# A transformer layer on eight cores: what TensorE waits for at the start of each group of heads

## The reference

```
a = layernorm(x)
Q = (a @ Wq.T + bq) * 128**-0.25 ; K = (a @ Wk.T + bk) * 128**-0.25 ; V = a @ Wv.T + bv
o = softmax(causal(Q @ K.T)) @ V            # head by head
x = x + layernorm(o @ Wo.T + bo)
h = bitlinear(layernorm(x), w_up)           # 2048 -> 4096
x = x + layernorm(bitlinear(relu(h)**2, w_down))
# bitlinear: activations quantised to 8 bits a row, weights to -1/0/1 times mean(|w|)
```

## Time and profile before

| | us |
|---|---|
| median of 2 runs | 6040.78 |
| the two runs | 6040.31 and 6041.24 |
| the profiled execution, its own time | 6060.33 |
| its span (slowest core, core 3) | 6058.8 |
| fastest core's span (core 0) | 5947.7 |

### The profile page before, as it was taken

How to read it: one execution, slowest core, us unless ns; L and a number is a source line. 1 busy time by engine, 2 the same in 40 slices (tenths; PEclk the granted TensorE clock), 3 DMA queues, 4 the chain that set the end, 5 groups by cost and what they waited for, 6 DMA issues and landing times.

```text
span 6058.8 us, 34280 instructions; the slowest of 8 cores (5947.7 to 6058.8 us)
## 1 busy us (share of the span) xinstructions
PE 2888.8 (48%) x10388; PEld 1096.4 (18%) x10388; DVE 1890.7 (31%) x2752; ACT 824.2 (14%) x929; POOL 378.2 (6%) x712
## 2 busy tenths in 40 slices
PE   0000474444744445644437444427847746675376
PEld 0000121111311112211113111102313312232132
DVE  1145022111131111212221311123456365363663
ACT  1100001111001112011110011110011112111210
POOL 0001110000110000100001100010000000000000
PEclk9999967766867777777778676657868868788688
DMA  5677421100121111201101110212134444433443
GB/s 92 99 224 233 92 43 35 39 32 33 39 60 35 35 35 34 49 35 35 35 35 39 46 35 35 89 61 103 49 104 115 118 132 111 157 108 97 130 114 118
DMA packets 358264, 471.07 MB, mean 78 GB/s; under 512 B 161473, under 2 KB 317121, under 8 KB 337345
## 3 DMA queue, kind: packets, MB, share of 16 engines
q0 software_dynamic: 68944, 251.21, 14.8%
q1 hardware_dynamic: 289138, 217.66, 13.3%
HBM read 385.39 MB, written 83.36 MB: 77 GB/s over the span
## 4 chain that ended last, share of the span: by engine, by line
PE 38%; DVE 17%; DMA 16%; ACT 12%; issue 6%; DVEq 4%; SPq 3%; POOL 3%; ACTq 0%; POOLq 0%
PE psB L1051 6%; ACT pt L643 6%; PE psB L473 4%; PE psB L435 4%; PE psB L1177 4%; PE psB L557 3%; DMA xt<-x 3%; DMA wqch<-wdnt 3%; DMA wqch<-wupt 3%; PE psB L795 3%; PE psB L664 2%; DVE tq_bf L387 2%; DMA qfm_ar<-qtile 2%; PE psB L505 2%; PE psA L630 2%
## 5 line engine op out<-in xcount | busy, mean ns | idle before, releaser
L1051 PE MATMUL psB<-wsl_f,qfm_ar 128*128 128x512 bf16 x2048 | 483.3, 401 | 350.0 <-DMA qfm_ar<-qtile 350.0
L1177 PE MATMUL psB<-wsl_f,qfm_ar 128*128 128x512 bf16 x2048 | 493.6, 406 | 267.4 <-DMA qfm_ar<-qtile 221.0
L643 ACT ACTIVATE pt<-psA,negC 128x1024 bf16<-128x1024 f32 x320 | 356.6, 1114 | 711.0 <-PE psA L634 708.7
L664 PE MATMUL psB<-pt,ones_bf 128*128 128x512 bf16 x320 | 149.8, 468 | 586.7 <-DVEq L91 325.8
L583 PE MATMUL psB<-sq_t,ones_f 128*128 128x512 f32 x128 | 89.4, 787 | 686.8 <-DVEq L91 686.8
L653 DVE TENSOR_TENSOR pt<-pt,strip 128x512 bf16<-128x512 bf16 x256 | 97.5, 422 | 1000.7 <-ACT pt L643 1000.7
L435 PE MATMUL psB<-y_fm,wsl 128*128 128x512 bf16 x1024 | 240.9, 402 | 180.2 <-DVEq L91 125.3
L1051 PEld LDWEIGHTS psB<-wsl_f,qfm_ar 128*128 128x128 bf16 x2048 | 208.3, 102 | 625.1 <-issue 409.4
L1177 PEld LDWEIGHTS psB<-wsl_f,qfm_ar 128*128 128x128 bf16 x2048 | 209.6, 103 | 551.3 <-issue 343.2
L795 PE MATMUL psB<-wo_bf,y_fm 128*128 128x512 bf16 x1024 | 268.4, 429 | 61.6 <-DVEq L91 55.3
L296 PE MATMUL psB<-smallA,ones_f 128*1 128x4 f32 x2 | 0.2, 166 | 623.8 <-DVEq L91 623.8
(11 more groups left out here) (160 smaller groups left out, 3232.1 us busy)
## 6 DMA issues: line engine op xcount, KB each, us to landing
wsl_f<-tup_sp SPq DMA_DIRECT2D x512, 128.0 KB, 2.7
wsl_f<-tdn_sp SPq DMA_DIRECT2D x512, 128.0 KB, 2.8
wch<-wupt POOLq DMA_DIRECT2D x16, 2048.0 KB, 9.0
wch<-wdnt POOLq DMA_DIRECT2D x32, 1024.0 KB, 5.5
wqch<-wupt POOLq DMA_DIRECT2D x32, 1024.0 KB, 5.6
wqch<-wdnt POOLq DMA_DIRECT2D x32, 1024.0 KB, 5.7
xt<-x SPq DMA_DIRECT2D x16, 1024.0 KB, 12.3
tup_sp<-tq_bf POOLq DMA_DIRECT2D x128, 128.0 KB, 2.2
```

Of the source, the lines that this page charges most:

```text
L643: exp_done[(hq, u)] = p.op("scalar", lambda e, sb=sb: e.activation(out=p_t[sb][:], in_=S2[sb][:, 0:1024], func=ACT.Exp, bias=negC[:], scal ...
L664: p.op("tensor", lambda e, sb=sb, u=u: e.matmul(PS[5][:, :], ones_bf[:, :], p_t[sb][:, 0:512], start=(u == 0), stop=False))
L1051: t_mm = p.op("tensor", lambda e, par=par, c=c, t=t, j=j: e.matmul(PS[par][:, :], q1fm[:, c * 512 + t * 128: c * 512 + (t + 1) * 128], wsl ...
L1177: t_mm = p.op("tensor", lambda e, par=par, c=c, t=t, s=s: e.matmul(PS[par][:, :], q2fm[:, c * 512 + t * 128: c * 512 + (t + 1) * 128], wsl ...
```

## The change

The two waits at the head of a group are replaced. For group 0 there is none. For the later groups TensorE waits for the reciprocal and for the output of the last attention block of the group before, and no longer for all that VectorE has been given.

```
@@ -411,8 +411,9 @@
     q_proj_last = {}
     hq = 0
     for grp in range(NG):
-        p.wait("tensor", SA, p.n(SA))
-        p.wait("tensor", SV, p.n(SV))
+        if grp > 0:
+            p.wait("tensor", SA, a_rec[hq - 1])
+            p.wait("tensor", SV, o_evac[hq - 1])
         wsl = wsl2[grp % 2]
         if grp == 0:
             lk = None
```

## The result

The changed kernel takes 5948.2 us in the median of 11 runs (5926.6 to 6039.1), the kernel before 6050.7 us in the median of 10 (6039.0 to 6109.1). The ratio is 0.9826 with a 95% interval of 0.9790 to 0.9861: 1.74% faster. The forecast was 5924.0 with a range up to 5942.0, so the time came out 24.2 us above the forecast and 6.2 us above the range. Ratios and means over the cores leave out executions in a second, slower state (one die over 1% longer than the other at a lower clock, or a time over 1.5% above the fastest), while medians and ranges hold all: without its one such execution, of 6039.1 us, the changed kernel's median is 5945.6, still 3.6 us above the range.

A forecast was written before the change was run, and what follows sets the result against it. The prediction took the kernel to be bound by waits, with TensorE's K projection held by VectorE at three group boundaries. Gains of 39.48, 38.63 and 38.72 us sum to 116.8; 6040.8 - 116.8 = 5924.0 us, range 5908 to 5942.

The forecast's parts named there:

- The stall and its releaser: At three group boundaries the K projection waited 125.3 us on VectorE, released by the third FFN-weight quantisation.
- Rival (d): Another event ending at the same time holds the K projection, so the time stays 6040.8 us; chance 0.02.
- The sum of 116.8 us: Gain from starting the K projection after the last attention output: 39.48, 38.63 and 38.72 us at the three boundaries.
- The moved work at nothing: Three quantisations under the K projection cost nothing, GpSimd issuing their last store 15.8 us before V weight loads are wanted.
- Rival (b): Contention stretches quantisations beyond the K projection, V loads 13 us late in all; gain 103.8, time 5937.0 us; chance 0.10.
- The slow start stays: The K projection still begins with eight matmuls at the low clock, costing 1.65 us per boundary as before.
- rival (a): With the gap gone, the K projection's slow start vanishes too: 121.7 us gained, time 5919.1 us; chance 0.13.
- a rise that comes later: At the K projection's start, a clock rise later than now was the only way to lose there; no size given.
- Rival (c): The whole K projection stays at the low clock, 49.8 us more per boundary; time 6073.4 us; chance 0.03.
- The base of the sum: Whole kernel's time before the edit, taken as the runs' median of 6040.8 us, from which the gain was subtracted.
- The range: Whole kernel's time between 5908 and 5942 us, with a few microseconds allowed for the spread between executions.
- The classes: Chances for the whole kernel: faster by over 2% 0.32, within 2% 0.66, slower by over 2% 0.02.

The follow-up runs named there:

- a fourth unit: Changed kernel with four FFN-weight quantisations instead of three at each group boundary, taken from the end of the attention stage; ratio 0.9730 to the kernel before.
- the fifth: Changed kernel with five FFN-weight quantisations instead of three at each group boundary, taken from the end of the attention stage; ratio 0.9764 to the kernel before.
- The filled gap: Kernel before with its wait kept and 170 thrown-away matmuls in TensorE's idle time at each boundary; ratios 1.0028 and 1.0014 to the kernel before.
- the three later comparisons: The changed kernel measured again, unedited, three times against the kernel before; ratios 0.9825, 0.9777 and 0.9799.

## Why the prediction missed, point by point

**The stall and its releaser: right.** The third quantisation held the K projection, and without it the projection starts 0.33 to 0.42 us after the output of the last block at each boundary of each core. Rival (d) falls.

**The sum of 116.8 us: right within what can be measured.** The trace shows 116.0 of waiting gone on core 7, 115.2 +- 2.8 in the means over the cores, 0.9813 (0.9790 to 0.9836) in the ratios against 0.9807 forecast. The time followed the wait when part of it was put back.

**The moved work at nothing, with a slack of 15.8 us: right.** GpSimd stood idle for 15.47 us; a fourth unit was all but free, the fifth was late. Rival (b) falls.

**The slow start stays: right, though it is 0.5 us longer at each boundary; rival (a) falls.** The projection began at 0.50 and took 58.1 us where the rows of before give 57.7. The prediction named this case, a rise that comes later, and put nothing on it. The filled gap shows the start from another side. On core 3 of its second profile dense matmuls ran at 1.00 up to 3.02 us ahead of the projection, and the projection still began at 0.50:

```profile
1500.00:1520.00 20.00, 20.00 (x94) 9.08 (x93) 4.78 (x3) 0.00 (x0) 5.33 (x10) 1.00 0.41 134
...
1525.00:1527.00 2.00, 0.00 (x0) 0.00 (x0) 2.00 (x1) 0.00 (x0) 0.00 (x0) 1.00 0.00 0
1527.50:1530.00 2.50, 2.50 (x7) 0.83 (x6) 0.00 (x0) 0.00 (x0) 2.13 (x4) 0.50 0.30 105
```

The filling left such a pause, of 2.0 to 5.2 us, at 38 of the 48 starts of the two profiles, and at 34 of them 6 to 13 matmuls were slow. At the other 10, all at 0.81 in the first profile, it left none or 0.3 us, and the projection went on at once at the clock that stood, as on core 5:

```profile
1491.88 44.67 PE L418 MATMUL psB<-y_fm,wsl 128*128 128x512 bf16 x170
1536.37 67.39 PE L442 MATMUL psB<-y_fm,wsl 128*128 128x512 bf16 x256
```

```profile
1530.00:1536.00 6.00, 6.00 (x24) 2.50 (x23) 4.39 (x3) 0.00 (x0) 0.92 (x2) 0.81 0.00 0
1536.50:1541.00 4.50, 4.50 (x19) 1.85 (x17) 0.00 (x0) 0.15 (x1) 0.71 (x2) 0.81 0.26 91
```

The advice of the Trainium skill that the prediction cited (page "TensorE: Matmul & The Clock Gate", section "Why this matters for your kernels") agrees with these starts: with no gap there was no slow start. What the prediction had right is that the edit is another case. It leaves 2.8 to 2.9 us of idleness behind sparse work, which at 85 of 96 starts of the changed kernel stands at 0.50 already, and all 96 starts are slow.

Rival (c), the whole projection at the low level, falls with the 187 matmuls in 40 us.

**The base of the sum: wrong.** The step that failed reads: "So the forecast is 6040.8 - 116.8 = **5924.0 us**". It took 6040.8, the median of two executions 0.9 us apart, for the kernel's time, though the profiled execution beside them took 19.55 us more. Ten executions have their median at 6050.7, and in the three later comparisons the kernel before had medians of 6078.0, 6068.7 and 6066.9 us. Nor was it that profiling makes an execution long: the profiled one of the changed kernel, at 5924.82, is *below* its median. Part of what made the profiled execution of before long stands in its trace. Core 3 in group 0, a window and the timeline of its K and V projections, and the same two of the changed kernel's core 7:

```profile
690.00:740.00 50.00, 50.00 (x192) 20.77 (x191) 0.00 (x0) 9.33 (x12) 0.00 (x0) 0.81 0.00 1
```

```profile
679.91 69.08 PE L435 MATMUL psB<-y_fm,wsl 128*128 128x512 bf16 x256 [54.92 <-DMA wsl<-wkt]
767.70 69.67 PE L473 MATMUL psB<-wsl,y_fm 128*128 128x512 bf16 x256
```

```profile
679.93 58.28 PE L436 MATMUL psB<-y_fm,wsl 128*128 128x512 bf16 x256 [54.94 <-DMA wsl<-wkt]
755.88 57.86 PE L474 MATMUL psB<-wsl,y_fm 128*128 128x512 bf16 x256
```

A granted clock of 0.81 through both projections cost that core 10.8 + 11.8 = 22.6 us. Of 24.2 us by which the forecast missed, 9.9 are the base (6050.7 - 6040.8). The other 14.3 are the distance of the two medians, 102.5 in place of 116.8; three further comparisons brought the pooled gain back to 113 us of 6050, so most of it was the spread of executions. The longer slow start is 1.5 us of it. At most some microseconds more can be a cost of the denser order; that part is open.

**The range: wrong in kind.** For the spread between executions I added "a few microseconds" to the bounds of the mechanism. In the first comparison the executions of the changed kernel that entered the ratio reach from 5924.8 to 5994.6 us. The clock of 0.81 is not the whole of it: the four profiled executions of that kernel never read it and took 5924.3 to 5960.8 us. The range had a width for each rival and none for the clock, though a trace with a projection of 69.08 us beside three of 57 was at hand.

**The classes.** 1.74% is within 2%, the likeliest of the three.

## What to carry to other kernels

A wait for "everything given out so far" costs what happens to stand last in the other engine's list; find that work, ask who reads its result, and wait for the event that guards the buffer. When such work is only moved, its slack can be read ahead from the timeline and tested by putting one unit more under the cover, and then one too many. Two equal times are no measure of the spread: if in one trace the same loop runs at two speeds, work out the difference and give it a place in the base and in the range.

## What the runs showed of the hardware

Between the clock's levels of 0.50 and 1.00 there is a third figure. In dense stretches that lasted a whole projection some executions show 0.81 and 192 matmuls in 50 us (0.260 us each), others of the same program 1.00 and 0.212 to 0.214 each. It came on neighbouring cores as a pair: in the profile of before, counted from each core's own start, first at 4156 and 4157 us on cores 0 and 1, at 686 on cores 2 and 3, at 2300 on cores 4 and 5 and at 1592 on cores 6 and 7. No core read it at any time in the four profiled executions of the changed kernel. Over all executions recorded a mean clock lower by 0.01 went with a span longer by 39 us. The Trainium skill, page "TensorE: Matmul & The Clock Gate", section "Part 1: The HAM clock gate", names a peak-current limiter that takes a whole die to 13/16 of the full clock, which would be 0.8125, once three of its cores run dense matmuls. The figure agrees. The rest is not borne out here: counted as above, the two pairs of one die first read 0.81 some 3470 and 710 us apart, and most dense stretches, of 58 us each, ran at 1.00 though all eight cores run the same program.

A second point: on core 3 of the filled kernel two idle microseconds read 1.00 in the window just ahead, and the next matmuls 0.50, so the level that stood before that pause of 3.02 us did not carry over to the burst behind it. Pauses of 2.0 to 2.7 us had the same end in five of five starts, 0.43 us for a matmul in place of 0.22 (0.26 at 0.81) from the second to fourth matmul on, and four pauses of 3.1 to 4.1 us did not. What decides between them no run here shows.
